# A four-layer conditioned network on one core: when TensorE is given attention's value products and the projection's transposes

## What is computed

```python
# scan layers (first and last)
xr, gate = split(x @ W_in.T, 2)                 # 512 -> 2 x 1024
xc = silu(causal_conv4(xr + t_emb))             # per channel, 4 taps
xn = layernorm(xc) * ln_g + ln_b                # over the 1024 channels
B, C, dt = split(xn @ W_xproj.T, 3)             # 16 each
...                                             # recurrence over the tokens
x = x + (y * silu(gate)) @ W_out.T

# attention layers (second and third), 16 heads of 32
x = normalise(x * s1)
q, k, v = x @ Wq.T, x @ Wk.T, x @ Wv.T          # each with a factor per batch and column
p = softmax(q @ k.T / sqrt(32))
x = x + (p @ v) @ Ww.T * w_dc + v @ Wu.T * u_dc
```

## Time and profile before

| | us |
|---|---|
| median of 3 runs | 3843.36 |
| lowest, highest | 3834.58, 3845.87 |
| the profiled execution's own time | 3847.87 |
| its span on the core | 3846.1 |
| TensorE busy | 3471.1 (90%) |
| VectorE busy | 2965.7 (77%) |
| ScalarE, GpSimd busy | 1345.1 (35%), 1855.8 (48%) |

### The profile page before, as it was taken

One profiled execution on the slowest core, in us unless ns is written; L12 is line 12 of the kernel. 1 busy time (PEld: TensorE's weight loads), 2 busy tenths in 40 slices (PEclk: granted clock), 3 DMA queues, 4 the chain that ended last, 5 costly groups with the idle time before them and its releaser, 6 DMA issues. The chain is left out here.

```text
span 3846.1 us, 63520 instructions
## 1 busy us (share of the span) xinstructions
PE 3471.1 (90%) x22068; PEld 2250.8 (59%) x22068; DVE 2965.7 (77%) x3172; ACT 1345.1 (35%) x2078; POOL 1855.8 (48%) x1384
## 2 busy tenths in 40 slices
PE   7999839999996899999999999997999938999998
PEld 6777614444444667777777777765777723444444
DVE  4766769999995777777777777753566759999998
ACT  3555511222122444334444444332455522112121
POOL 2555646555553124444444444342455555555554
PEclk9999969999997899999999999998999978999999
DMA  3566675555553233222322222223466675555553
GB/s 126 216 249 251 255 245 213 200 203 213 207 203 124 86 107 108 75 78 80 113 83 91 83 81 72 72 75 117 173 252 238 229 289 193 216 196 203 203 204 142
DMA packets 288590, 631.06 MB, mean 164 GB/s; under 512 B 33472, under 2 KB 35904, under 8 KB 288224
## 3 DMA queue, kind: packets, MB, share of 16 engines
q1 hardware_dynamic: 281200, 615.49, 45.3%
q10 hardware_dynamic: 7104, 11.81, 0.8%
HBM read 390.75 MB, written 241.70 MB: 164 GB/s over the span
## 5 line engine op out<-in xcount | busy, mean ns | idle before, releaser
L1201 DVE CUSTOM_DVE_ANT_0 l3r_g<-l3r_g,l3r_pv,l3r_cf 128x1024 f32<-128x1024 f32 x512 | 642.4, 1341 | 31.6 <-PE l3r_pv L1010 23.7
L1201 DVE CUSTOM_DVE_ANT_0 l0r_g<-l0r_g,l0r_pv,l0r_cf 128x1024 f32<-128x1024 f32 x512 | 642.1, 1340 | 23.6 <-PE l0r_pv L1010 15.5
L142 PE MATMUL l1h_ps_p<-l1h_xh,l1c_wh 128*128 128x512 f32 x768 | 322.3, 420 | 5.6 <-issue 3.5
L144 PE MATMUL l1h_ps_p<-l1h_xl,l1c_wh 128*128 128x512 f32 x768 | 308.3, 401 | 0.0
L2187 POOL TENSOR_TENSOR l1h_st<-l1h_veps 128x1 f32<-128x1 f32 x64 | 35.3, 552 | 561.8 <-DVE l1h_veps L2045 561.8
L143 PE MATMUL l1h_ps_p<-l1h_xh,l1c_wl 128*128 128x512 f32 x768 | 305.3, 397 | 0.0
L1799 ACT ACTIVATE l1h_pt<-l1h_ps_t 128x512 f32<-128x512 f32 x256 | 151.0, 590 | 369.8 <-PE l1h_ps_t L1672 369.8
L1025 PE MATMUL l3r_py<-l3r_g,l3r_cd 128*32 128x512 f32 x2048 | 254.5, 613 | 0.8 <-issue 0.8
L1025 PE MATMUL l0r_py<-l0r_g,l0r_cd 128*32 128x512 f32 x2048 | 253.2, 613 | 1.2 <-ACT l0r_y L1110 1.2
L2085 DVE TENSOR_TENSOR l1h_e<-l1h_e,l1h_mx 128x1024 f32<-128x1024 f32 x128 | 216.4, 1691 | 4.4
L2104 DVE TENSOR_TENSOR l1h_vt<-l1h_ps_p,l1c_dc 128x512 f32<-128x512 f32 x64 | 44.2, 691 | 220.0 <-PE l1h_ps_p L144 220.0
(11 more groups left out here) (400 smaller groups left out, 8963.1 us busy)
## 6 DMA issues: line engine op xcount, KB each, us to landing
l0r_x<-xhl_s SPq DMA_DIRECT2D x128, 512.0 KB, 5.5
l3r_x<-xhl_s SPq DMA_DIRECT2D x128, 512.0 KB, 5.6
xhl_s<-l0a_xo SPq DMA_DIRECT2D x116, 512.0 KB, 4.6
xhl_s<-l3a_xo SPq DMA_DIRECT2D x116, 512.0 KB, 4.6
gate_s<-l0a_gate SPq DMA_DIRECT2D x64, 256.0 KB, 2.6
l0r_dx<-dx_s SPq DMA_DIRECT2D x32, 512.0 KB, 7.8
l0r_gate<-gate_s SPq DMA_DIRECT2D x32, 512.0 KB, 8.6
l0r_crow<-feed_s SPq DMA_DIRECT2D x64, 256.0 KB
```

The lines of the kernel that those rows point to most:

```text
L142: pe.matmul(out, wh, xh, start=first, stop=False)
L144: return pe.matmul(out, wh, xl, start=False, stop=last)
L1201: dve._custom_dve(bass.dve_ops.TENSOR_ADD_SAT, out=g[:, t, j, :], in0=g[:, (t - 1) % TS, j, :], in1=pv[(k.off + t + j) % 3][:, :], s0=cf[: ...
```

## The change

In the attention phase TensorE runs `values(g, 0)` no longer in front of `turn(g, 1)` but in front of `values(g, 1)`, and `values(g, 2)` no longer in front of `turn(g, 3)` but in front of `values(g, 3)`. In the projection phase `turn` moves from the end of the even step, behind its gate product, to the odd step, between its input product and its gate product; in tile 7 it moves behind the input product of the odd step. Instructions are neither added nor taken away, and the lists of VectorE, ScalarE, GpSimd and SyncE are the same as before.

```diff
             for T in range(1, NT - 1):
                 for it in range(KI):
                     project_x(T, it)
+                    if it % 2 == 1:
+                        turn(TB * (T - 1) + it // 2)
                     if rows and it == KI - 1:
                         turn_x(T + 1, TB - 1)
                     project_gate(T, it)
-                    if it % 2 == 0:
-                        turn(TB * (T - 1) + it // 2)
                     if it == 1:
                         xproj(T - 1)
...
             T = NT - 1
             for it in range(KI):
                 project_x(T, it)
-                if it % 2 == 0:
+                if it % 2 == 1:
                     turn(TB * (T - 1) + it // 2)
...
                 if sooner(p, "K"):
                     project(p, Q, "Q", q_mm)
-                values(g, 0)
                 turn(g, 1)
                 if burst:
                     turn_x(p, "X3")
...
                     project(p, Q, "Q", q_mm)
+                values(g, 0)
                 values(g, 1)
                 turn(g, 2)
                 if not sooner(p, "Q"):
                     project(p, Q, "Q", q_mm)
                 if extra(p):
                     next_sum_rows(p)
-                values(g, 2)
                 turn(g, 3)
                 if not sooner(p, "K"):
                     project(p, K, "K", k_mm)
                 if extra(p):
                     next_add_rows(p)
+                values(g, 2)
                 values(g, 3)
                 turn_v(p)
```

## The result

| | median us | lowest to highest |
|---|---|---|
| before | 3841.15 | 3834.58 to 3845.87 |
| changed | 3793.69 | 3790.56 to 3801.17 |

The account below looks back on a forecast made before the run. TensorE's list was taken to set the pace in attention and projection. 27.0 + 10.0 + 6.5 + 10.8 = 54.3 us gave 3793.6 from the profiled execution, 3789.1 from the median; 3792 was taken, own range 3779 to 3806, with rivals to 3816.

Parts of the forecast that it names:

- Values: Attention: each pair of value runs put together saves 0.30 us (bounds 0.10 and 0.30), 27.0 us in all.
- a second run of values is not cheap: Attention: only the way in is saved, 0.10 us a pair; 23.2 us less than forecast, about 3815; chance 0.07.
- One of the prediction's signs of being wrong: Attention: the forecast is wrong if line 1672 waits for line 1799; no size given for this sign.
- The first turn's wait: Projection, five tiles a layer: TensorE's wait for the SiLU goes, 1.4 us a tile in first layer, 1.3 in last.
- VectorE becomes the bound: Projection: VectorE waits for `turn` in each odd step, 0.4 us; 22 of 27.3 us come back, about 3814; chance 0.07.
- The wait for xl: First layer's projection: step 0's input product comes later and finds `xl` ready, saving 0.6 us in each of five tiles.
- Tile 7: Projection: VectorE's wait for the second input product goes; 5.3 us in first layer, 5.5 in last, together 10.8.

Follow-up runs that it names:

- the kernel with attention alone: Only the attention reordering of `values`, against the kernel before, projection as before: 3820.31 us, ratio 0.9946.
- the kernel with the projection alone: Only the projection's move of `turn`, against the kernel before, attention as before: 3816.63 us, ratio 0.9936.
- the kernel with the first pair alone: Only `values(g, 0)` moved down to `values(g, 1)`, against the kernel before: 3834.77 us, ratio 0.9985.

## Why the prediction was right, and where not

**Forecast and range.** 3792 against 3793.69, inside its own range. Of the 54.3 us of the sum, about 47 came. That the forecast is within 2 us is luck: the sum was 7 us too large, and 3792 amounts to taking it from 3846.3, which is 5 above the median before (3841.15). The range, and the mechanism in attention, at the first `turn` and in tile 7, were right by the runs. The terms:

**Values.** 0.30 a pair in the sum, 0.28 to 0.30 measured; the second run 0.22 in the sum, 0.23 measured; regular periods 0.58 shorter (0.60), bursts 0.07 (0.08). The value taken from the scores was right, and the rival "a second run of values is not cheap" falls. The estimate from the Trainium skill's page "TensorE: Matmul & The Clock Gate", Single matmul latency, was 0.11 us a pair; the runs show 0.29, and the measurement decides. The Trainium skill's page gives these 128 cycles in its breakdown for the half clock, 1.2 GHz; by that clock an estimate is 0.107 us a switch and 0.21 a pair, which is still short of the 0.29.

43 x 0.58 + 15 x 0.07 is 26.0. Periods can be measured from 6 to 62, since no scores follow those of 63. Six of them (15, 16, 31, 38, 47 and 48, most of them where a loop turns back or the layer changes) differ from run to run; the 51 steady ones took 1001.6 us instead of 1025.5, 24.0 less, as 40 x 0.58 + 11 x 0.07 asks. The six took 134.1 us after and 131.6 before; with the same attention list they took 129.9 in the kernel with attention alone and 129.4 to 133.5 in four others. From the last scores to the end of the stage it was 57.8 us instead of 61.3; with the same list it was 57.8 to 60.1 in the other five, and 59.5 in the kernel with the projection alone, which has the list of before. So these two differences go from run to run.

One of the prediction's signs of being wrong did appear, though in few periods: line 1672 waits for line 1799 eight times, 7.1 us in all, in periods 1, 2, 4, 5, 38, 48 and 63 (twice). In its place line 1682 waits for line 1799 less than before: four times and 5.3 us, where it was ten and 10.9.

**The first turn's wait.** 1.4 us a tile in the first layer: 54.97 to 53.55, 1.42. In the last layer 1.3: 56.03 to 54.67, 1.36, and tile 1 gained 0.86 besides, which the sum had not and which comes from the other three turns. No other wait took its place, and VectorE's wait for `turn` in the odd steps is 0.2 and costs nothing: the rival "VectorE becomes the bound" falls.

**The wait for xl: the step that failed.** The sum counted 5 x 0.6 = 3 us because "the product comes 0.8 later by itself". It took the end of step 7's input product as what `xl` hangs on. But the `evacuate` of step 7 does not wait for that product, in either trace: it starts behind VectorE's own work (the last two rows here, and 293.57 behind 292.97 + 0.68 before). In the trace the chain begins earlier, with the gate product of step 5, and goes over POOL. Changed kernel, the links on ScalarE, POOL and VectorE in turn:

```profile
281.04 0.60 ACT L497 ACTIVATE l0a_gate<-l0a_pg 128x512 f32<-128x512 f32 x1 [1.64 <-PE l0a_pg L144]
281.53 0.62 ACT L478 ACTIVATE l0a_xh<-l0a_xt 128x512 fp32r<-128x512 f32 x1
282.05 1.05 ACT L530 ACTIVATE l0a_xo<-l0a_xn 128x1024 fp32r<-128x1024 f32 x1
...
288.96 1.15 ACT L515 ACTIVATE l0a_xn<-l0a_xn,l0s_stat 128x1024 f32<-128x1024 f32 x1
...
283.18 2.40 POOL L758 TENSOR_TENSOR l0a_xo<-l0a_xn,l0a_xo 128x1024 fp32r<-128x1024 f32 x1 [1.00 <-ACT l0a_xo L530]
...
283.44 2.69 DVE L610 TENSOR_TENSOR l0a_xl<-l0a_xt,l0a_xh 128x512 fp32r<-128x512 f32 x1
286.05 0.68 DVE L621 TENSOR_TENSOR l0a_pad<-l0a_pxr,l0a_temb 128x512 f32<-128x512 f32 x1
...
289.83 0.68 DVE L610 TENSOR_TENSOR l0a_xl<-l0a_xt,l0a_xh 128x512 fp32r<-128x512 f32 x1
290.43 0.68 DVE L621 TENSOR_TENSOR l0a_pad<-l0a_pxr,l0a_temb 128x512 f32<-128x512 f32 x1
```

The gate's SiLU of step 5 lets ScalarE go on to line 530, that POOL's line 758; VectorE's split is held 0.55 beyond POOL's end and delays the `evacuate` of step 6; on that hang ScalarE's next steps down to line 515, then POOL's line 744, and 0.55 after its end the last `xl`. The SiLU starts 17.40 us before the next tile's first `evacuate` in the changed kernel (281.04 and 298.44) and before it (284.17 and 301.57). Between that gate product and the product that waits, TensorE has the same work in both orders, since `turn` only moves from step 6 to step 7. So by this chain nothing could be gained there, and nothing was. The experiments show its last link, POOL's add; the links before it are read from the trace and were not tried. Most of the rest of the 4.3 us that the layer fell short is its start: tile 1 began 0.8 us later, and tile 0, which took 66.2 us instead of 64.5, takes 63.0 to 68.5 in the other kernels.

**Tile 7.** First to third `evacuate` 15.12 to 9.79 in the first layer and 15.25 to 9.78 in the last: 5.3 and 5.5, as in the sum, at full clock.

**Where the recurrence's 5.5 us are from.** Busy time of that stage, in the kernel before, in the changed one, and in the kernel with the first pair alone, which has the projection of before:

```profile
498.20:1205.70 707.50, 609.33 (x4112) 276.73 (x4112) 667.14 (x539) 139.65 (x231) 392.86 (x326) 0.95 0.55 199
```

```profile
487.10:1200.10 713.00, 616.07 (x4112) 277.90 (x4112) 667.38 (x539) 139.65 (x231) 393.13 (x326) 0.94 0.55 198
```

```profile
499.20:1213.70 714.50, 614.94 (x4112) 277.76 (x4112) 667.42 (x539) 139.76 (x231) 393.49 (x326) 0.94 0.55 197
```

VectorE's work is the same; TensorE is busy 5.6 to 6.7 us more at a mean clock of 0.94 instead of 0.95. Over all 14 kernels the stage lies between 705.8 and 714.5 whatever was changed, so this is most likely chance of the execution; with one profile of each kernel that is not shown. The same holds for the last layer's start: its tile 0 took 68.3 us before and 66.1 after, and 63.1 to 68.6 in the others, which covers 2.2 of the 3.8 us that the layer gave above the sum.

## What to carry over

Read a switch between forms of matmul from starts, and put runs of one form together: it paid 0.29 us each time until the engine that feeds the run was late, and then that engine's list had to be moved as well. A wait that stays after its supposed cause is gone hangs on another chain: follow it back over every engine, and look for two instructions that always end at a fixed distance. A place where the engine waits anyway is free for work; moving work away from there costs its full price elsewhere.

## What the runs showed of the hardware

VectorE's subtraction of two operands in SBUF (line 610) is held while POOL adds or subtracts. When it started during POOL's instruction it took 0.81 to 2.70 us instead of 0.68, and it ended 0.55 us after POOL's in 24 of 24 cases in tiles 1 to 6, before and after. When it started first, it took 0.68, and the add that POOL began 0.36 us into it took 2.59 to 2.60 us instead of 2.38 to 2.40, in 12 of 12; in the kernel that moved the add no add starts within a split, and it takes 2.37 to 2.43.

The Trainium skill's page "SBUF — State Buffer", section "Who interferes with whom", says that a VectorE instruction with two SBUF inputs contends with a GpSimd instruction that reads SBUF, and that the later one blocks; the 24 cases agree, and in the 12 others it is POOL that is delayed.

With one operand in PSUM there is no such hold. In the last layer the same subtraction (line 607) reads the turned x from PSUM (`pp`), and the 24 splits that start beside POOL, 12 before and 12 after, last 0.68 to 0.69 us. One of them, with POOL's instruction:

```profile
2874.21 0.68 DVE L607 TENSOR_TENSOR l3a_xl<-l3a_pp,l3a_xh 128x512 fp32r<-128x512 f32 x1
...
2873.94 2.40 POOL L758 TENSOR_TENSOR l3a_xo<-l3a_xn,l3a_xo 128x1024 fp32r<-128x1024 f32 x1 [1.47 <-ACT l3a_xo L530]
```

The taps of line 632, with `pad` in SBUF and `pacc` in PSUM, are not held either: 51 of the 144 in tiles 1 to 6 of the changed kernel start beside POOL and last 0.74 to 0.76 us, as the 93 others do.
